# Routing stage of a graph and expert layer: the second normalisation on GpSimd, the logits copy and the epsilon on ScalarE

## The reference

```python
edge_index = jnp.stack([src, dst])
xn = _layernorm(x, axis=-1)
x = x + _L0_gnn_ref(xn, edge_index, ...) + _L0_mix_ref(xn[None], ...)[0]
x = x + _L0_ffn_ref(_layernorm(x, axis=-1)[None], L0_ffn_router_w, ...)[0]

def _layernorm(x, axis=-1, eps=1e-05):
    m = jnp.mean(x, axis=axis, keepdims=True)
    v = jnp.var(x, axis=axis, keepdims=True)
    return (x - m) / jnp.sqrt(v + eps)

# in _L0_ffn_ref
logits = flat @ router_w.T
probs = jax.nn.softmax(logits, axis=-1)
topk_probs, topk_idx = jax.lax.top_k(probs, TOP_K)
```

## Time and profile before

| quantity | value |
|---|---|
| time, median of 3 runs | 3320.83 us |
| lowest and highest | 3319.59 and 3324.13 us |
| the profiled execution's own time | 3308.1 us |
| its span, first to last instruction | 3306.0 us |
| mean granted TensorE clock | 0.859 of 2.4 GHz |

### The profile page before, as it was taken

How to read it: one execution, slowest core, us unless ns; L and a number is a source line. 1 busy time by engine, 2 the same in 40 slices (tenths; PEclk the granted TensorE clock), 3 DMA queues, 4 the chain that set the end, 5 groups by cost and what they waited for, 6 DMA issues and landing times. The chain is left out here.

```text
span 3306.0 us, 46533 instructions
## 1 busy us (share of the span) xinstructions
PE 2443.2 (74%) x10229; PEld 1689.5 (51%) x10230; DVE 1739.1 (53%) x6232; ACT 1227.6 (37%) x3908; POOL 1141.3 (35%) x1101
## 2 busy tenths in 40 slices
PE   0116888863778778878777787760099999999998
PEld 0113444432556556656555565540067666776765
DVE  7775444434777777777777777771022222222222
ACT  6001222213555555555555555210023332333332
POOL 0000000007666666666666666006511111111111
PEclk9999899875787787786877877985599999999999
DMA  3000111152333333333333336557611211111121
GB/s 141 0 0 32 62 64 64 59 206 72 91 90 90 90 91 90 91 90 90 90 90 91 90 90 85 159 163 234 191 29 30 32 31 31 31 31 32 30 32 26
DMA packets 156692, 258.73 MB, mean 78 GB/s; under 512 B 28097, under 2 KB 109122, under 8 KB 155766
## 3 DMA queue, kind: packets, MB, share of 16 engines
q0 software_dynamic: 62592, 143.11, 18.7%
q1 hardware_dynamic: 93942, 113.93, 10.9%
HBM read 183.18 MB, written 73.75 MB: 78 GB/s over the span
## 5 line engine op out<-in xcount | busy, mean ns | idle before, releaser
L745 POOL DMA_INDIRECT arena<-table,arena x880 | 877.8, 997 | 1180.9 <-DVE arena L826 741.3
L772 PE MATMUL psum<-arena 128*128 128x257 f32 x1760 | 704.2, 533 | 281.4 <-issue 157.8
L772 PEld LDWEIGHTS psum<-arena 128*128 128x128 f32 x1760 | 377.7, 252 | 504.1 <-issue 423.0
L867 DVE SCALAR_TENSOR_TENSOR arena<-arena,psum 128x257 f32 x880 | 423.3, 481 | 351.4 <-remote 249.1
L1262 PE MATMUL psum<-arena 128*128 x1696 | 534.3, 458 | 1.4 <-ACT arena L1337 0.7
L1364 DVE TENSOR_TENSOR arena<-psum,arena 128x341 f32<-128x341 f32 x212 | 109.0, 514 | 641.0 <-ACT arena L1319 454.6
L1395 POOL DMA_INDIRECT out<-arena x106 | 164.7, 1554 | 755.1 <-ACT arena L1345 747.5
L1262 PEld LDWEIGHTS psum<-arena 128*128 128x128 f32 x1696 | 305.7, 190 | 162.3 <-issue 38.1
L795 ACT ACTIVATE arena<-arena 128x128 f32<-128x128 bf16 x880 | 281.0, 390 | 154.5 <-DVE arena L881 108.9
L1295 PE MATMUL psum<-arena 128*128 x1272 | 312.9, 388 | 1.1 <-ACT arena L1327 1.1
L808 ACT ACTIVATE arena<-arena 128x128 f32<-128x128 bf16 x880 | 281.1, 390 | 7.1
(11 more groups left out here) (316 smaller groups left out, 3133.5 us busy)
## 6 DMA issues: line engine op xcount, KB each, us to landing
arena<-table,arena POOLq DMA_INDIRECT x880
expert_in<-arena SPq DMA_DIRECT2D x1, 13674.0 KB
arena<-expert_in SPq DMA_DIRECT2D x106, 129.0 KB, 2.0
mix_inputs<-arena SPq DMA_DIRECT2D x100, 128.0 KB, 1.8
arena<-mix_inputs SPq DMA_DIRECT2D x50, 256.0 KB, 2.9
arena<-xn SPq DMA_DIRECT2D x98, 128.0 KB
arena<-in_w SPq DMA_DIRECT2D x6, 1364.0 KB
out<-arena SPq DMA_DIRECT2D x51, 128.0 KB, 2.2
```

What stands on the lines that cost most here:

```text
L745: pool.indirect_dma_start(rows_in[j][:, q * TW:(q + 1) * TW], None, table_d[:, :], bass.IndirectOffsetOnAxis(ap=col_all[:, t:t + 1], axis=0))\
L772: mm(psum[4 + q][:, 0:C + 1], weight[b][:, q * P:(q + 1) * P], rows_in[g][:, q * TW:q * TW + C + 1], start=True, stop=True).then_inc(S("pr ...
L867: v.scalar_tensor_tensor(here, here, alpha[(j - 5) % RING][:, q:q + 1], psum[4 + q][:, 0:C + 1], ALU.mult, ALU.add).then_inc(S("acc_done"), 1)
```

## The change

Four edits in the routing stage, and nothing elsewhere:

1. The normalisation (L1088 before) moves from VectorE to GpSimd, into a new function `route_pool` with the same lag of three tiles, called between stages 2 and 3. It has the same waits for the reuse of `xn2` as before.
2. The copy of the logits (L1078 before) moves from VectorE to ScalarE, with the same lag of six tiles, behind the copy of the transposed tile.
3. The addition of epsilon (L1070 before) is gone; the square root adds it as its bias, from a column `eps_col` that is set once, and waits for `mv_done` instead of `var2_ready`.
4. `mv2` and `std2` have four buffers instead of two, and `bn_aggr` of tile t waits for `xn2_ready` of two tiles less.

```diff
-        mv2 = [take(2, 2) for _ in range(2)]
-        std2 = [take(2, 2) for _ in range(2)]
+        mv2 = [take(2, 2) for _ in range(4)]
+        std2 = [take(2, 2) for _ in range(4)]
+        eps_col = take(2, 1)
...
-                    act.wait_ge(S("var2_ready"), t + 1)
-                    nc.scalar.activation(std2[b][:, 1:2], std2[b][:, 0:1], ACT.Sqrt).then_inc(S("std2_ready"), 1)
+                    act.wait_ge(S("mv_done"), t + 1)
+                    nc.scalar.activation(std2[(j - 2) % 4][:, 1:2], mv2[(j - 2) % 4][:, 1:2], ACT.Sqrt, bias=eps_col[:, :])\
+                        .then_inc(S("std2_ready"), 1)
...
+                if live(i, 6, NT):
+                    bl, tl = (j - 6) % 2, i - 6
+                    act.wait_ge(S("logits_done"), after("logits_done", tl + 1))
+                    nc.scalar.activation(logits[:, ds(tl * NE, NE)], psum[4 + bl][:, 0:NE], ACT.Copy).then_inc(S("logits_ready"), 1)
...
+        def route_pool(pool):
+
+            def step(i, j, k):
+                if live(i, 3, NT):
+                    place, t3 = (j - 3) % 4, i - 3
+                    pool.wait_ge(S("rstd2_ready"), t3 + 1)
+                    if due(t3 - 3):
+                        pool.wait_ge(S("xn2_turned"), t3 - 3)
+                    if t3 >= 4:
+                        pool.wait_ge(S(f"xn2_out{place}"), after(f"xn2_out{place}", t3 // 4 * 16))
+                    nc.gpsimd.tensor_scalar(xn2[place][:, :], acc[:, ds(t3 * TW, C)], mv2[place][:, 0:1], std2[place][:, 0:1],
+                                            ALU.subtract, ALU.mult).then_inc(S("xn2_ready"), 1)
+
+            quads(pool, step, 3)
...
+            v.memset(eps_col[:, :], EPS)
...
-                    if due(t - 1):
-                        dve.wait_ge(S("xn2_ready"), after("xn2_ready", t - 1))
+                    if due(t - 3):
+                        dve.wait_ge(S("xn2_ready"), after("xn2_ready", t - 3))
...
-                if live(i, 2, NT):
-                    dve.wait_ge(S("mv_done"), t + 1)
-                    v.tensor_scalar(std2[b][:, 0:1], mv2[b][:, 1:2], EPS, None, ALU.add).then_inc(S("var2_ready"), 1)
...
-                if live(i, 6, NT):
-                    bl, tl = (j - 6) % 2, i - 6
-                    dve.wait_ge(S("logits_done"), after("logits_done", tl + 1))
-                    v.tensor_copy(logits[:, ds(tl * NE, NE)], psum[4 + bl][:, 0:NE]).then_inc(S("logits_ready"), 1)
...
-                    v.tensor_scalar(xn2[(j - 3) % 4][:, :], acc[:, ds(t3 * TW, C)], mv2[bt][:, 0:1], std2[bt][:, 0:1],
-                                    ALU.subtract, ALU.mult).then_inc(S("xn2_ready"), 1)
```

More of the change, by code:

```diff
@@ L1025, in step @@
                     nc.scalar.activation(xn2t[bt][:, :], psum[2 + bt][:, 0:C], ACT.Copy).then_inc(S("xn2t_ready"), 1)
-            quads(act, step, 4)
+                if live(i, 6, NT):
+                    bl, tl = (j - 6) % 2, i - 6
+                    act.wait_ge(S("logits_done"), after("logits_done", tl + 1))
+                    nc.scalar.activation(logits[:, ds(tl * NE, NE)], psum[4 + bl][:, 0:NE], ACT.Copy).then_inc(S("logits_ready"), 1)
+            quads(act, step, 6)
             act.wait_ge(S("exponents_ready"), 1)
@@ L1057, in step @@
                     dve.wait_ge(S("st_done"), t + 1)
-                    if due(t - 1):
-                        dve.wait_ge(S("xn2_ready"), after("xn2_ready", t - 1))
+                    if due(t - 3):
+                        dve.wait_ge(S("xn2_ready"), after("xn2_ready", t - 3))
                     dve.sem_inc(S("vector_steps"), 1)
-                    v.bn_aggr(mv2[b][:, :], st2[:, :]).then_inc(S("mv_done"), 1)
+                    v.bn_aggr(mv2[(j - 2) % 4][:, :], st2[:, :]).then_inc(S("mv_done"), 1)
                 if live(i, 1, NT):
@@ L1067, in step @@
                         .then_inc(S("x2_ready"), 1)
-                if live(i, 2, NT):
-                    dve.wait_ge(S("mv_done"), t + 1)
-                    v.tensor_scalar(std2[b][:, 0:1], mv2[b][:, 1:2], EPS, None, ALU.add).then_inc(S("var2_ready"), 1)
                 if live(i, 3, NT):
-                    bt, t3 = (j - 3) % 2, i - 3
+                    place, t3 = (j - 3) % 4, i - 3
                     dve.wait_ge(S("std2_ready"), t3 + 1)
-                    v.reciprocal(std2[bt][:, 0:1], std2[bt][:, 1:2]).then_inc(S("rstd2_ready"), 1)
-                if live(i, 6, NT):
-                    bl, tl = (j - 6) % 2, i - 6
-                    dve.wait_ge(S("logits_done"), after("logits_done", tl + 1))
-                    v.tensor_copy(logits[:, ds(tl * NE, NE)], psum[4 + bl][:, 0:NE]).then_inc(S("logits_ready"), 1)
[L1079 to L1087, removed]
-                    v.tensor_scalar(xn2[(j - 3) % 4][:, :], acc[:, ds(t3 * TW, C)], mv2[bt][:, 0:1], std2[bt][:, 0:1],
-                                    ALU.subtract, ALU.mult).then_inc(S("xn2_ready"), 1)
-            quads(dve, step, 6)
+                    v.reciprocal(std2[place][:, 0:1], std2[place][:, 1:2]).then_inc(S("rstd2_ready"), 1)
+            quads(dve, step, 3)
             dve.wait_ge(S("logits_ready"), after("logits_ready", NT))
@@ L1642, in _ @@
             phase(pool, 2)
+            route_pool(pool)
             phase(pool, 3)
```

## The result

The changed kernel takes 3335.94 us (median of 8 runs, 3328.38 to 3342.53) against 3321.61 us of the kernel before (8 runs, 3319.59 to 3324.13). The ratio is 1.0043, 95% interval 1.0032 to 1.0054: slower by 14.3 us, clear of the 0.2% that I had set as no change, and outside the range, which ended at 3331 us.

The account below looks back on a forecast made before the run. The prediction took a three-tile loop through SP's in-order queue, with the normalisation before the load, as the bound. +1.8 - 1.5 - 0.3 - 1.0 = -1.0 us on 3320.8 gave 3319.8 us, range 3312 to 3331.

Parts of the forecast that it names:

- The round over three tiles through SP's queue: Routing stage: half sum, normalisation, stores, load, landing, product, next half sum; 5.86 us before, 5.35 + h + X after.
- X: Time of the normalisation on GpSimd, inside the round; taken as 0.55 us, ends 0.31 and 1.23.
- The term +1.8 us: Stage cost of the normalisation on GpSimd: 14.7 x (h + X - 0.51), ends -2.5 and +15.0 us.
- The upper end: Longest normalisation on GpSimd considered: three times VectorE's 0.41, 1.23 us.
- The rule against the change: Skill's rule: elementwise work about twice as slow on GpSimd; X 0.82, stage +5.7 us, 3324 us, chance 0.2.
- h: Handoff from VectorE's reciprocal to GpSimd's normalisation; taken as 0.08 us, ends 0.03 and 0.3.
- The other parts, -2.8 us: Everything but the moved normalisation in the round: -1.5 for VectorE, -0.3 for epsilon, -1.0 for the tail.
- VectorE's relief, epsilon and first tiles: Stage: fewer ready tiles waiting for VectorE, -1.5 us (0 to -3); earlier square root in first tiles, -0.3 once.
- The tail: From the last half sum to the first instruction behind the copies, 9.9 us: -1.0 us, between -2 and +1.
- The slower one: SP's wait for GpSimd's normalisation before the load: h + X above 1.15, up to +12.2 us, 3333 us, chance 0.2.
- The faster one, shorter landings: Loads in the stage land after 2.6 us instead of 2.9: with other gains -9.7 us, 3311 us, chance 0.2.
- The base: Start of the forecast: median 3320.8 us, to which the -1.0 was carried from the profiled execution, 12.7 us below it.

Follow-up runs that it names:

- the late store: SP stores the normalised tile one step later (tile i-6 instead of i-5): ratio 0.9995 in the changed kernel, 1.0002 in the kernel before.
- loads first: On top of the late store, SP issues the load ahead of the stores, x2's one step later: changed kernel 0.9958 and 0.9979, kernel before 0.9984.
- the third set: Later set of runs in which the unchanged changed kernel ran again against the kernel before: 3326.49 us against 3314.82, ratio 1.0036.

## Why the prediction was wrong

- **What bounds the kernel: right for the change.** The round over three tiles through SP's queue was read correctly. With the true X its length comes out to 0.03 us (6.70 against 6.67), and the late store takes the loss away. That a shorter round would make the kernel before faster is not shown by any run: the late store shortened its way to the load by 0.09 us only, and with loads first the landing grew by as much as was saved.
- **X, the step that failed.** The mechanism held and one term of the sum was too small. The prediction says "I take X = 0.55, the row that is nearest in kind", from the affine select and the memset extrapolated to 256 columns. It measured 1.22. The term +1.8 us should have been +11.9. Both rows were poor neighbours: the fixed part came from a memset of one column, 0.089 us, where the two widths now give 0.37; the slope came from one affine select of half the width, 1.8 ns a column, where they give 3.3. Neither row has two scalars per lane among its operands; whether that is what costs was not tried. The upper end that I had set, 1.23, was nearly exact, but I had given it 0.2 and let the range stop short of its 3333 us.
- **The rule against the change.** Both the row and the rule, which gave 0.82, came out too low. The Trainium skill ("GPSIMD Engine Reference", Engine selection) has GpSimd about twice as slow for two inputs and roughly at line rate for one; this one-input operation took 3.0 times VectorE's time (1.219 against 0.413 us). The measurement decides; only the direction of the rule held.
- **h: right**, 0.10 against 0.08.
- **The other parts, -2.8 us.** VectorE's relief, epsilon and first tiles: with the normalisation back on VectorE -2.3 us (-5.6 to +0.7), consistent. The tail was taken at -1.0 and came out at +1.2 and +0.5 us in the two profiles of the changed kernel; with the normalisation on VectorE it is 9.5 us, so that it is GpSimd that lengthens it. Here X has a second price: the last four normalisations stand one behind the other on GpSimd (4.95 us), and the transposes wait for them.
- **The rivals.** The slower one, GpSimd's normalisation holding back the load, is what happened, at its upper end: 3333 us forecast for it, 3335.94 measured. That TensorE's transposes come late as well is seen (5.3 us, 12 times) but not shown to cost anything. The faster one, shorter landings, went the other way: 3.1 us in the median instead of 2.9.
- **The base.** Carrying the sum to the median was right: the lead of the profiled execution sat ahead of the routing.
- What the runs leave over: +9.1 us by the sum with the true X against 14.3 (10.6 to 17.9) and, in the third set, 11.9 (7.6 to 16.3). The tail accounts for 1.5 to 2.2 of it; the rest is within the intervals.

## What to carry to other kernels

An idle engine is free only if the moved work is not in the chain that sets the pace: here VectorE was relieved of a fifth of its busy time in the stage (93.9 to 72.8 us) and the kernel became slower, because the product of that work stood before a load in an in-order DMA queue. Look first at what stands behind what in the queue; moving one store by one step undid the loss as fully as moving the normalisation back. Issuing a transfer costs time in that queue too: two stores hold a load back by 0.89 us though nothing waits. And an operation that no row shows should be given the range of its bounds, not the value of the nearest row, when the loss hangs on it linearly.

## What was not expected of the hardware

- GpSimd's `tensor_scalar` with two per-lane scalars on 128x256 f32: 1.219 us, on 128x128 0.792 us, against VectorE's 0.413 us for 256 columns. On 128x256 it hardly scatters (1218 to 1228 ns).
- ScalarE's square root of one column became longer with its bias from a column of its own:

```profile
L1020 ACT ACTIVATE arena<-arena x50: 279/295/296, 2115.5 to 2233.4; 128x1 f32<-128x1 f32 x50
```

```profile
L1031 ACT ACTIVATE arena<-psum x50: 167/170/187, 2123.2 to 2241.1; 128x8 f32<-128x8 f32 x50
```

  0.295 us where it was 0.203, while the copy of eight columns out of PSUM takes only 0.170. With the normalisation alone moved, where the square root has no such bias, it takes 0.203 again. It was covered here, as ScalarE waited before it.
- There are stretches of half clock, which lengthen a product. TensorE's product of tile 24 in the changed kernel, and the stretch it falls in (granted clock 0.58, between the levels 1.2 and 2.4 GHz):

```profile
2167.83 1.97 PE L989 MATMUL psum<-arena 128*128 128x256 f32 x4 [2.20 <-DMA arena<-mix_inputs]
```

```profile
2168.00:2172.00 4.00, 4.00 (x16) 3.47 (x16) 1.45 (x5) 0.75 (x3) 1.04 (x1) 0.58 0.56 193
```

  Four passes take 1.97 us there instead of 1.13. This one follows a wait of 2.20 us, others follow none: with the late store in the changed kernel, a product at 2214.70 us takes 2.08 us without a wait before it. Such stretches come in all profiles, at other tiles each time. The two profiles of the kernel before differ by 0.06 us a tile at granted clocks of 0.97 and 0.89; how much of it is the clock was not separated.
